# Memory attention, masked attention and gated experts of a decoder in one pipelined stage instead of three

## The reference

```
x = layernorm(x + ffn0(x))          # here only: weigh and add each token's two expert rows
# L1 attention ("memory"): linear attention with decay, M = 64
q, k, v = x @ Wq, x @ Wk, x @ Wv;  g = sigmoid(x @ Wg + bg)
S_t = decay * S_(t-1) + outer(g k_t, g v_t);  y_t = q_t @ S_t
x = layernorm(x + y @ Wo + bo)
# L1 cross attention ("masked"): one head of width 256, keys and values from ctx
sim = where(mask, -1e9, (x Wq' + bq) (ctx Wk' + bk)')
x = layernorm(x + softmax(sim) @ (ctx Wv' + bv) @ Wo' + bo)
# L1 ffn ("gated"): 8 experts, gates below 0.1 cut, rest normalised
w = softmax(x @ gate_w + gate_b) * (. >= 0.1);  w = w / sum(w)
x = layernorm(x + sum_e w_e * (x @ expert_w[e] + expert_b[e]))
```

## Time and profile before

| | us |
|---|---|
| three runs: median (lowest, highest) | 2352.73 (2348.17, 2362.13) |
| profiled execution, its time | 2355.41 |
| its span, first to last instruction | 2353.4 |
| memory stage, from 1584 to 1792 | 208 |
| masked stage, from 1792 to 2052 | 260 |
| gated stage, from 2052 to the end | 301 |

### The profile page before, as it was taken

How to read it: one execution, slowest core, us unless ns; L and a number is a source line. 1 busy time by engine, 2 the same in 40 slices (tenths; PEclk the granted TensorE clock), 3 DMA queues, 4 the chain that set the end, 5 groups by cost and what they waited for, 6 DMA issues and landing times. The chain is left out here.

```text
span 2353.4 us, 30152 instructions
## 1 busy us (share of the span) xinstructions
PE 1923.2 (82%) x8625; PEld 1154.0 (49%) x8625; DVE 1340.0 (57%) x3286; ACT 943.7 (40%) x2525; POOL 627.3 (27%) x806
## 2 busy tenths in 40 slices
PE   7785857888888888748849999994665999689998
PEld 5453524455545444426635665652444666444443
DVE  2482448898989889724422222226772455546666
ACT  3322659888988888613312222211111333100000
POOL 2000025555555555404420000006542011100000
PEclk9897979999999999967659999996887999989999
DMA  5524631121112122022231213204332021110110
GB/s 194 204 85 152 239 123 50 55 66 48 60 58 63 50 63 64 22 87 81 80 133 63 80 64 107 72 27 131 117 98 83 33 85 63 47 45 26 36 36 18
DMA packets 173999, 188.56 MB, mean 80 GB/s; under 512 B 18596, under 2 KB 157083, under 8 KB 172864
## 3 DMA queue, kind: packets, MB, share of 16 engines
q1 hardware_dynamic: 166592, 162.76, 21.1%
q0 software_dynamic: 6144, 16.18, 2.0%
q10 hardware_dynamic: 1152, 8.39, 0.8%
...
## 5 line engine op out<-in xcount | busy, mean ns | idle before, releaser
L746 POOL TENSOR_SCALAR xa_probs<-xa_probs,xa_rinv 128x512 f32<-128x512 f32 x512 | 344.6, 692 | 293.9 <-DVE xa_rinv L791 293.9
L911 PE MATMUL xa_ps_t<-xa_ident,xa_probs 128*128 128x128 f32 x2048 | 327.1, 286 | 59.3 <-POOL xa_probs L746 53.4
L764 ACT ACTIVATE xa_probs<-xa_ps_s,xa_nmax 128x512 f32<-128x512 f32 x512 | 351.9, 708 | 26.5 <-DVE xa_nmax L795 26.1
L911 PEld LDWEIGHTS xa_ps_t<-xa_ident,xa_probs 128*128 128x128 f32 x2048 | 234.4, 144 | 239.0 <-POOL xa_probs L746 84.0
L795 DVE TENSOR_REDUCE xa_nmax<-xa_ps_s 128x2 f32<-128x1024 f32 x256 | 307.2, 1200 | 39.7 <-PE xa_ps_s L903 38.1
L681 ACT ACTIVATE xa_probT<-xa_ps_t 128x512 f32<-128x512 f32 x368 | 226.5, 621 | 61.7 <-PE xa_ps_t L911 52.9
L2341 PE MATMUL ga_ps_e<-ga_ew,ga_xT 128*128 128x512 f32 x512 | 235.0, 608 | 0.0
L903 PE MATMUL xa_ps_s<-xa_k,xa_q 96*128 96x512 bf16 x512 | 159.5, 394 | 53.5 <-ACT xa_probs L764 33.0
L2281 DVE SCALAR_TENSOR_TENSOR ga_acc<-ga_ps_e,ga_gate,ga_acc 128x256 f32<-128x256 f32 x256 | 123.9, 484 | 79.0 <-PE ga_ps_e L2341 70.9
L2341 PEld LDWEIGHTS ga_ps_e<-ga_ew,ga_xT 128*128 128x128 f32 x512 | 95.2, 193 | 114.3 <-issue 103.0
L1406 ACT ACTIVATE ex_hid<-ex_ps_g 128x512 f32<-128x512 f32 x64 | 38.3, 598 | 254.5 <-PE ex_ps_u L1459 254.5
...
## 6 DMA issues: line engine op xcount, KB each, us to landing
...
```

The costliest lines, as they stand in the source:

```text
L746: ins = pool.tensor_scalar(probs[h % NP][:, t, :], probs[h % NP][:, t, :], rinv[h % 2][:, t:t + 1], 1.0, ALU.mult, ALU.mult)
L764: ins = act.activation(probs[h % NP][:, t, :], ps_s[j][:, t % 2, :], ACT.Exp, bias=nmax[h % 2][:, t:t + 1], accum_out=rsum[h % 2][:, t:t + 1])
L911: ins = pe.transpose(ps_t[t % 2][:, i * P:(i + 1) * P], probs[(h - 2) % NP][:, i, t * P:(t + 1) * P], ident[:, :])
```

## The change

The three stages become one, `stage_tail` (names ta_). It is written out, without loops, as 11 steps. In step s the engines work on memory attention of batch s, masked attention of batch b = s-1, the gates and expert units 0 to 9 of batch c = s-2, and units 10 to 15 of batch d = s-3. A `unit` is the product of one tile with two experts; `g_add` is its two additions. x3, x4 and x5 stay in SBUF; the loads and stores of x4 and x5 through DRAM go away. The stages share PSUM: `ps_w` (two banks) is used for all turns, the keys, the outputs of memory, logits, gates and bias; `ps_s` for projections, triangle scores and masked scores; `ps_v` for memory's values, side products and turned exps; `ps_o` for readings, masked values and masked output; `ps_e` has two buffers instead of four. Many tiles that had two buffers have one (x3T, qT, kT, oT, x4T, gT, v, gateT). The copy of the turned exps moves from VectorE to ScalarE. Indices aren't copied ahead of the gather. The expert biases are added for a whole batch (`g_begin`) instead of for each tile. The fold of the masked weights and the loads of all weights stand at the start of the stage. `has(b)` is 0 <= b < B.

```diff
-        stage_memory(nc, a, route_w, route_i)
-    stage_xattn1(nc, a)
-    stage_gated(nc, a)
+        stage_tail(nc, a, route_w, route_i)
```

POOL, the start and the step:

```diff
+            gather(0)
+            for w in (m_wq[:, :, :], m_wk[:, :, :], m_wv[:, :, :], m_wo[:, :]):
+                pool.memset(w, 0.0).then_inc(pad_up, 1)
...
+            def step(s_):
+                if has(s_ - 2):
+                    pool.wait_ge(x_var, s_ - 1)
+                    power(rx, vex, x_root)
+                if has(s_):
+                    if s_ == 0:
+                        pool.wait_ge(c_ld, 128)
+                    pool.wait_ge(m_x3, s_ + 1)
+                    wait(pool, m_z2, s_)
+                    pool.tensor_tensor(x3b[:, :, :], x3[s_ % 2][:, :, :], row(m_bo[:, :]).to_broadcast([P, T, D]), ALU.add).then_inc(m_x3b, 1)
+                if has(s_ - 1):
+                    if s_ == 1:
+                        pool.wait_ge(b_ld, 16)
+                    pool.wait_ge(m_x4, s_)
+                    wait(pool, x_z, T * (s_ - 1))
+                    pool.tensor_tensor(x4b[:, :, :], x4[(s_ - 1) % 2][:, :, :], row(bo[:, :]).to_broadcast([P, T, D]), ALU.add).then_inc(m_x4b, 1)
+                if has(s_):
+                    pool.wait_ge(b_var, s_ + 1)
+                    power(rb, veb, b_root)
+                if has(s_ - 3):
+                    pool.wait_ge(g_var, s_ - 2)
+                    power(rg, veg, g_root)
+                if has(s_ + 2):
+                    pool.wait_ge(m_z, s_ + 1)
+                    gather(s_ + 2)
+                if has(s_ + 1):
+                    pool.wait_ge(m_var, s_ + 2)
+                    power(rm, vem, m_root)
```

ScalarE's step:

```diff
+            def step(s_):
+                b, c = s_ - 1, s_ - 2
+                if has(s_):
+                    m_turned(s_)
+                    m_copies(s_)
+                    m_gates(s_)
+                if has(c):
+                    g_turned(c)
+                    g_exps(c)
+                if has(s_):
+                    m_read(s_)
+                if has(c):
+                    g_gates(c)
+                if has(b):
+                    x_turned(b)
+                    x_side(b)
+                    x_keys(b)
+                    x_scores(b, 0)
+                    x_exps(b, 0)
+                    x_scores(b, 1)
+                    x_exps(b, 1)
+                    x_exT(b, 0)
+                    x_scores(b, 2)
+                    x_exT(b, 1)
+                    x_exps(b, 2)
+                    x_scores(b, 3)
+                    x_exT(b, 2)
+                    x_exps(b, 3)
+                    x_exT(b, 3)
```

VectorE's additions and its step:

```diff
+            def g_add(c, k):
+                if not has(c):
+                    return
+                n, t = U * c + k, k // (E // 2)
+                if k == 0:
+                    dve.wait_ge(g_acc0, c + 1)
+                    dve.wait_ge(g_gate, 2 * c + 2)
+                dve.wait_ge(g_e, n + 1)
+                for i in range(2):
+                    e = 2 * (k % (E // 2)) + i
+                    wait(dve, g_acc, 2 * n + i)
+                    dve.scalar_tensor_tensor(acc[c % 2][:, t, :], ps_e[n % 2][:, i, :], gate[c % 2][:, t, e:e + 1], acc[c % 2][:, t, :],
+                                             ALU.mult, ALU.add).then_inc(g_acc, 1)
...
+            def step(s_):
+                b, c, d = s_ - 1, s_ - 2, s_ - 3
+                g_add(d, 10)
+                if has(c):
+                    x_finish(c)
+                g_add(d, 11)
+                if has(s_):
+                    m_gated(s_)
+                g_add(d, 12)
+                if has(s_):
+                    m_faded(s_, 0)
+                    m_faded(s_, 1)
+                if has(c):
+                    g_soft(c, True)
+                if has(s_):
+                    m_faded(s_, 2)
+                g_add(d, 13)
+                if has(s_):
+                    m_faded(s_, 3)
+                g_add(d, 14)
+                if has(c):
+                    g_soft(c, False)
+                if has(s_):
+                    m_back(s_)
+                g_add(d, 15)
+                if has(d):
+                    g_norm(d)
+                if has(s_):
+                    m_finish(s_)
+                if has(d):
+                    g_finish(d)
+                if has(b):
+                    x_values(b, 0)
+                    x_values(b, 1)
+                if has(c):
+                    g_begin(c)
+                more = has(s_ + 1)
+                if has(b):
+                    x_maxima(b, 0)
+                if more:
+                    m_front(s_ + 1, 0)
+                g_add(c, 0)
+                if has(b):
+                    x_maxima(b, 1)
+                if more:
+                    m_front(s_ + 1, 1)
+                g_add(c, 1)
+                g_add(c, 2)
+                if more:
+                    m_front(s_ + 1, 2)
+                if has(b):
+                    x_maxima(b, 2)
+                g_add(c, 3)
+                if has(b):
+                    x_out(b, 0)
+                if more:
+                    m_front(s_ + 1, 3)
+                g_add(c, 4)
+                if has(b):
+                    x_maxima(b, 3)
+                g_add(c, 5)
+                if has(b):
+                    x_out(b, 1)
+                if more:
+                    m_front(s_ + 1, 4)
+                g_add(c, 6)
+                g_add(c, 7)
+                if more:
+                    m_front(s_ + 1, 5)
+                if has(b):
+                    x_out(b, 2)
+                g_add(c, 8)
+                if more:
+                    m_front(s_ + 1, 6)
+                if has(b):
+                    x_out(b, 3)
+                g_add(c, 9)
+                if has(b):
+                    x_norm(b)
```

PE's masked values, a unit, and its step:

```diff
+            def x_values(b, half):
+                if half == 0:
+                    pe.wait_ge(cld[b % 2], 32 * (b // 2) + 32)
+                    wait(pe, m_oT, min(b + 2, B))
+                    wait(pe, x_z, T * b)
+                else:
+                    pe.wait_ge(x_vs, 2 * b + 1)
+                for t in range(2):
+                    for h in range(DH):
+                        ins = pe.matmul(ps_vx[:, t, :], cT[b % 2][:, h, (2 * half + t) * P:(2 * half + t + 1) * P], wvo[:, h, :],
+                                        start=(h == 0), stop=(h == DH - 1))
+                ins.then_inc(x_v, 1)
...
+            def unit(c, k):
+                if not has(c):
+                    return
+                n, t, e = U * c + k, k // (E // 2), 2 * (k % (E // 2))
+                wait(pe, g_acc, 2 * n - 2)
+                for h in range(DH):
+                    ins = pe.matmul(ps_e[n % 2][:, :, :].rearrange("p e d -> p (e d)"), x5T[c % 2][:, h, t * P:(t + 1) * P],
+                                    ew[:, h, e:e + 2, :].rearrange("p e d -> p (e d)"), start=(h == 0), stop=(h == DH - 1))
+                ins.then_inc(g_e, 1)
+
+            def step(s_):
+                b, c, d = s_ - 1, s_ - 2, s_ - 3
+                if has(s_):
+                    m_turn(s_)
+                unit(d, 10)
+                if has(s_):
+                    m_project(s_)
+                unit(d, 11)
+                if has(s_):
+                    m_values(s_)
+                if has(c):
+                    g_turn(c)
+                unit(d, 12)
+                if has(s_):
+                    m_scores(s_, 0)
+                    m_scores(s_, 1)
+                if has(c):
+                    g_logits(c)
+                if has(s_):
+                    m_reading(s_, 0)
+                    m_scores(s_, 2)
+                unit(d, 13)
+                if has(s_):
+                    m_reading(s_, 1)
+                    m_scores(s_, 3)
+                    m_reading(s_, 2)
+                unit(d, 14)
+                if has(s_):
+                    m_reading(s_, 3)
+                unit(d, 15)
+                if has(s_):
+                    m_out(s_)
+                if has(b):
+                    x_values(b, 0)
+                if has(c):
+                    g_turn_gates(c)
+                if has(b):
+                    x_turn(b)
+                    x_values(b, 1)
+                    x_side(b)
+                    x_keys(b)
+                if has(c):
+                    g_bias(c)
+                if has(b):
+                    x_scores(b, 0)
+                unit(c, 0)
+                if has(b):
+                    x_scores(b, 1)
+                unit(c, 1)
+                unit(c, 2)
+                if has(b):
+                    x_exT(b, 0)
+                    x_scores(b, 2)
+                unit(c, 3)
+                if has(b):
+                    x_exT(b, 1)
+                    x_out(b, 0)
+                unit(c, 4)
+                if has(b):
+                    x_scores(b, 3)
+                unit(c, 5)
+                if has(b):
+                    x_exT(b, 2)
+                    x_out(b, 1)
+                unit(c, 6)
+                unit(c, 7)
```

(7 more changed lines are left out.)

1143 lines of the change are left out of this document (466 added, 677 removed).

## The result

After the change the kernel takes 2388.5 us (median of 4 runs, 2372.9 to 2389.6), before it 2355.3 us (4 runs beside them, 2348.2 to 2362.1). The ratio is 1.0126, 95% interval 1.0073 to 1.0178: slower by 33 us, where the forecast was 40 us faster, 2313 in a range of 2270 to 2355. One of the later runs of before, beside the experiments e5 to e8, took 6703.6 us and is left out of every ratio. The profiled execution of after took 2388.6 us on a span of 2386.8.

The account below looks back on a forecast made before the run. PE was taken as the bound in the masked and gated stages, idle in memory's chain. Start, steps and end summed to 724.2 us instead of 764.5, 40.3 less, giving 2313 us, range 2270 to 2355.

Parts of the forecast that it names:

- The gap of 6.2 us: PE idle behind x4's turn, waiting for VectorE to take out masked values; clock loss after it 2.1 us, at most 4.5.
- step 2: First step with gated work, units 0 to 9, beside memory and masked attention: 36 + 32.8 = 68.6 us.
- step 8: Late step without memory attention, the other stages still running: 66.5 us.
- the five full steps: Steps 3 to 7, with all stages at work: 80.2 us each, 401 us together.
- The steady step of the new stage: One full step walked engine by engine: ends at 78.1 us, 80.2 with the clock loss added.
- PE hardly waits; here the units do what they are there for: First half of a full step: expert products cover PE's waits up to memory's output at 25.0 us.
- Start, steps 0 and 1: Stage start to first turn 37 us, memory alone 36, memory and masked without units 57.
- PE is not stopped: Second half of a full step: VectorE's additions ready 0.4 to 3 us before PE asks for the buffer.
- rival b: VectorE falls behind in the second half, missed turns cost PE 1.5 us each; 2376 us, chance 0.11, part way 0.11.
- Rival (c): Waits across stages put them one after the other, units find no gap; step 87 us, time 2361, chance 0.06.
- Rival (a): PE is covered: short VectorE queue, clock doesn't fall; step 71.3 us, time 2254, chance 0.12.
- Table loads: ScalarE changes between sigmoid and exp twice a step, 1.28 us a load; 1 us in all, 5 by the skill's 2.66.

Follow-up runs that it names:

- e5: Changed kernel with VectorE making the masked values early and the keys put before the side products; 2260.0 us, 0.9623 of before.
- e8: Changed kernel with masked values early on VectorE and side products 128 columns wide instead of 2; 2283.2 us, 0.9713 of before.
- e6: Changed kernel with unused spare products on PE in both waits, behind x4's turn and between keys and bias; 2312.1 us, 0.9837 of before.
- e1: Changed kernel with VectorE making the masked values early, ahead of the gated norm; 2286.3 us, 0.9695 of before.
- e2: Changed kernel with seven unused spare products on PE behind x4's turn (three where no expert products stand); 2323.7 us, 0.9871 of before.
- e3: Changed kernel with unused spare products of 512 and 320 columns only between keys and bias; 2358.6 us, 1.0012 of before.
- e10: Changed kernel with three unused spare products in each step behind x4's turn; 2358.1 us, 1.0040 of before.
- e4: Changed kernel with the keys before the side products on PE and ScalarE; 2339.1 us, 0.9922 of before.
- e7: Changed kernel with side products 128 columns wide instead of 2, constant weight 0.5; 2354.9 us, 1.0029 of before.

## Why the prediction was wrong, point by point

**The step that failed: "half of that is lost, 1.7 and 2.6, 2.1 in the mean. The gap of 6.2 us is of that size; I add 2.1, upper bound 4.5".** The term measured 9.4 to 9.8 us in each full step: 9.4 is after's step less that of e6, whose clock stays up (88.5 and 79.1), 9.6 the busy time against e5's (80.0 and 70.4), 9.8 half of what ran at the low level. e1 and e2 show that the larger part goes with the gap, e3 that 3.4 go with the wait for the keys' copy. With 9.6 in this place the forecast would have been 2313 + 5 x 7.5 = 2351, almost the whole gain gone. In step 2 and step 8 the sum had no such term of its own, and there the clock takes some 11 us each, half of about 22 us of busy PE at the low level. By stretches, the five full steps are 42 us too long for the forecast, step 2 is by 11.7 and step 8 by 12.5 (79.0 for 66.5), together 66 of the 67.3. Of the 42, some 5 are not the clock's but a walk that was 0.9 us a step too short.

**What was wrong in it.** I chose the rows by the length of the gap. By e10 and after, that length hardly matters in the full steps once the clock falls. The work behind matters more: behind the gaps of the earlier trace rows stood products of 512 to 128 columns (the first of them in the row of before below), and the level lasted 3.4 and 5.3 us, as it does in e4 (5.4) and e7 (5.9). In the new stage there stand the second half of the values and the 2-column side products, and it lasts 12.8. The row that resembled this was the fold, with one-column products in it, 9 us at 0.50 with PE busy throughout, and I had it, as an upper bound only. Its half, 4.5, was too small as well: the first level alone costs 6.4 us, half of 12.8, and a second fall, from the bias on, 3.4 us by e3, had no place in the sum.

```profile
1672.30 2.07 PE L1787 MATMUL me_ps_o<-me_aT,me_gv 128*128 128x512 f32 x2 [4.93 <-issue]
```

**"The steady step of the new stage", walked at 78.1 without the clock: right to 0.9 us.** All waits came where and as long as said: 6.06 for 6.2, 1.45 for 1.4, 0.77 for 0.7. e6, which takes the clock out, has 79.0.

**"PE hardly waits; here the units do what they are there for": right** up to the output. What PE lacked was one cover, in the very place where the walk found none.

**Start, steps 0 and 1: right** to 1.8 us. **Step 2:** 80.3 for 68.6. Its gap is 2.79 us, and it too was followed by a low level, as these rows of after show (its second half of the values, and the stretch behind it):

```profile
1752.08 3.78 PE L2213 MATMUL ta_ps_o<-ta_wvo,ta_cT 128*128 128x256 f32 x8 [2.79 <-DVE ta_v L1906]
```

```profile
1751.50:1764.00 12.50, 11.92 (x30) 8.29 (x31) 1.22 (x2) 0.26 (x1) 6.44 (x7) 0.50 0.29 84
```

**"PE is not stopped" in the second half (against rival b): right.** PE is busy 29.00 of 29.00 us from 2130 to 2159. **Rival (c)**, a step of 87 by stages in a row, has nearly the measured step for another reason: PE is covered up to the output, as walked, so it isn't that one. A time near a rival's is no proof of it.

**Rival (a): its mechanism can be had.** It needed a short queue on VectorE and a clock that doesn't fall, and I held against it that seven groups lie in a fixed order. The order is fixed by hand, and e5 only changes places in it: the masked values on VectorE, the keys on PE and ScalarE.

**Table loads: the row was right.** In after, ScalarE's load and the activation behind it, in step 2:

```profile
1730.80 1.28 ACT L1742 ACT_TABLE_LOAD   x1
1732.09 0.26 ACT L1742 ACTIVATE ta_g<-ta_ps_v,ta_bg 128x4 f32<-128x4 f32 x1
```

The activation starts 0.01 us behind the load's end: a switch costs 1.3 us. The Trainium skill's 2.66 (ScalarE: Activation LUTs, What ACT_TABLE_LOAD costs) isn't borne out here.

**The range** held neither the time nor the mechanism's true bound. Its chance for slower, 0.11, was all in rival (b), and none in the clock, though the clock was the one term whose price came from rows of other work.

The Trainium skill (TensorE: Matmul & The Clock Gate, HAM oscillation — how this bites in real kernels) tells of a kernel in which a wait that returns in every tile leaves the engine slow at the head of each, and counts some 1.67 us at the low level for each wait. This case's trace agrees with the pattern, step by step, and not with the size: 12.8 us at 0.50 behind one wait.
